# A recurrence and a mixture of experts on one core: the downs six units behind the ups, a rebuilt head, and five downs as three rounded passes

## What is computed

```python
xw = einsum('ntd,dh->nth', x, Wx) + b                 # 32 rows, 32 steps, 128 features
h_t = tanh(xw_t + h_(t-1) @ Wh)                       # a scan over the 32 steps
xf = h.reshape(-1, 128)                               # 1024 tokens
xn = xf * rsqrt(mean(xf * xf) + EPS) * norm_scale
vals, idx = top_k(xn @ wg + bg, 4)                    # 16 experts, 4 per token
gate = one_hot(idx) weighted by softmax(vals)
u = einsum('th,ehd->etd', xn, w1) + b1                # per expert: the up product
a, b = minimum(u[..., ::2], 7), clip(u[..., 1::2], -7, 7)
s = a * sigmoid(1.702 * a) * (b + 1)
y = einsum('eti,eih->eth', s, w2) + b2                # per expert: the down product
out = x + h + sum over e of gate[t, e] * y[e, t]
```

## Time and profile before

| | us |
|---|---|
| median of three runs | 108.16 |
| profiled execution | 107.47 |
| its span, first to last instruction | 105.7 |
| TensorE busy | 98.3 (93%) |
| VectorE, ScalarE, GpSimd busy | 67.2, 61.7, 64.7 |
| TensorE's share of the chain that ended last | 82% |

### The profile page before, as it was taken

One profiled execution on the slowest core, in us unless ns is written; L12 is line 12 of the kernel. 1 busy time (PEld: TensorE's weight loads), 2 busy tenths in 40 slices (PEclk: granted clock), 3 DMA queues, 4 the chain that ended last, 5 costly groups with the idle time before them and its releaser, 6 DMA issues.

```text
span 105.7 us, 1704 instructions
## 1 busy us (share of the span) xinstructions
PE 98.3 (93%) x549; PEld 83.6 (79%) x549; DVE 67.2 (64%) x179; ACT 61.7 (58%) x143; POOL 64.7 (61%) x77
## 2 busy tenths in 40 slices
PE   7778899989999999999999979999999999999980
PEld 2557789978999999999999958888777777777660
DVE  0302357976827996589787997668566556666740
ACT  3354836999755586667736646666555666655400
POOL 6004447997890995639963799689544566544400
PEclk9999999999999999999999999999999999999999
DMA  2999920007930000895048911995100000000003
GB/s 66 224 378 338 374 92 0 0 9 254 398 147 3 0 6 6 212 372 212 5 141 228 366 67 20 274 364 207 34 6 0 3 0 0 0 0 0 0 0 99
DMA packets 5000, 12.97 MB, mean 123 GB/s; under 512 B 752, under 2 KB 1792, under 8 KB 4992
## 3 DMA queue, kind: packets, MB, share of 16 engines
q1 hardware_dynamic: 4672, 12.69, 35.5%
q10 hardware_dynamic: 320, 0.18, 0.6%
HBM read 12.28 MB, written 0.59 MB: 122 GB/s over the span
## 4 chain that ended last, share of the span: by engine, by line
PE 82%; ACT 7%; DMA 2%; DVE 2%; POOL 2%; issue 2%; POOLq 0%; DVEq 0%; ACTq 0%
PE psA L806 20%; PE psB L806 19%; PE psY L836 12%; PE psR L836 7%; PE psR L753 5%; PE psY L753 3%; PE psM L836 3%; PE psR L848 2%; DMA wx_x_sb<-in_wx_x 2%; PE psR L745 2%; PE psM L760 2%; ACT small_h L450 2%; ACT psA L494 2%; PE psM L767 1%; ACT psA L503 1%
## 5 line engine op out<-in xcount | busy, mean ns | idle before, releaser
L414 POOL TENSOR_TENSOR actg<-act,gate_cols 128x512 f32<-128x512 f32 x31 | 39.4, 1281 | 12.5 <-DVE act L713 10.7
L696 DVE TENSOR_SCALAR lin<-psB,one_b1b 128x256 f32<-128x256 f32 (+1 forms) x48 | 26.0, 568 | 18.8 <-PE psB L806 18.8
L494 ACT ACTIVATE psA<-psA,lim_b1a 128x256 f32<-128x256 f32 (+1 forms) x48 | 23.8, 513 | 23.2 <-PE psA L806 23.1
L713 DVE SCALAR_TENSOR_TENSOR act<-lin,psA 128x512 f32<-128x512 f32 x32 | 22.0, 686 | 1.8 <-ACT psA L503 0.6
L503 ACT ACTIVATE psA<-psA,limit_col 128x512 f32<-128x512 f32 x32 | 21.1, 659 | 0.8
L806 PE MATMUL psA<-xn_hi,w_hi 128*128 128x256 f32 (+1 forms) x48 | 18.9, 394 | 0.2
L836 PE MATMUL psY<-actg,w_sb 128*128 128x256 f32 x64 | 17.2, 391 | 0.8 <-POOL actg L414 0.8
L806 PE MATMUL psB<-xn_hi,w_hi 128*128 128x256 f32 (+1 forms) x48 | 16.0, 333 | 0.0
L806 PE MATMUL psB<-xn_lo,w_hi 128*128 128x256 f32 (+1 forms) x48 | 15.6, 324 | 0.0
L806 PE MATMUL psB<-xn_hi,w_lo 128*128 128x256 f32 (+1 forms) x48 | 15.5, 323 | 0.0
L806 PE MATMUL psA<-xn_hi,w_lo 128*128 128x256 f32 (+1 forms) x48 | 15.5, 323 | 0.0
(11 more groups left out here) (87 smaller groups left out, 133.7 us busy)
## 6 DMA issues: line engine op xcount, KB each, us to landing
gate_cols<-gate_rows SPq DMA_DIRECT2D x16, 512.0 KB, 5.7
w_sb<-in_w SPq DMA_DIRECT2D x4, 512.0 KB, 7.3
w_sb<-in_w SPq DMA_DIRECT2D x4, 256.0 KB, 8.3
wx_x_sb<-in_wx_x SPq DMA_DIRECT2D x1, 320.0 KB, 5.9
wx_x_sb<-in_wx_x SPq DMA_DIRECT2D x2, 128.0 KB, 2.7
out<-yT SPq DMA_DIRECT2D x2, 128.0 KB, 4.3
out<-yT SPq DMA_DIRECT2D x1, 192.0 KB, 1.9
small_h<-in_small ACTq DMA_DIRECT2D x1, 105.0 KB, 2.8
```

Of the source, the lines that this page charges most:

```text
L414: nc.gpsimd.tensor_tensor(by_pair(actg[:, u % SUM_DEPTH, w]), by_pair(act[:, u % ACT_DEPTH, w]), gate_block(u, w), ALU.mult).then_inc(actg ...
L494: last = nc.scalar.activation(psA[u % 2][:, o], psA[u % 2][:, o], ACT.Relu, scale=-1.0, bias=lim_b1a[:, e0 + k:e0 + k + 1])
L696: last = nc.vector.tensor_scalar(lin[:, v % 2, o], psB[v % 2][:, o], one_b1b[:, e0 + k:e0 + k + 1], LIMIT + 1.0, ALU.add, ALU.min)
L713: nc.vector.scalar_tensor_tensor(act[:, v % ACT_DEPTH, 0:w], lin[:, v % 2, 0:w], 1.0 - LIMIT, psA[v % 2][:, 0:w], ALU.max, ALU.mult).then_ ...
```

## The change

`LAG` goes from 4 to 6, `POOL_LAG` from 2 to 3, and the buffers of `act` and `actg` from 6 and 5 to 8 and 6. With this, `add_h` of chunk 0 and the first down of chunk 1 move from slot 12 to slot 14, and the tail has six downs. The tail's two rounds are 256 and 256 columns where they were 384 and 128.

In the head, tile 1's x·Wx goes to `psX`, as do its sums of squares, with semaphores of their own. The products of tiles 1 to 6 are issued in the head (in steps' shadows or around the sums); only tile 7 comes later, in slot 10, where tiles 5 to 7 came together in slot 6. ScalarE rounds all of w1 before unit 0. In the first six slots the gate transposes and ScalarE's gate copies stand earlier in their slots. `gates_scale` is two scalar multiplications in place of one tensor product.

In units 17, 19, 21, 23 and 25 the down is three passes of fp32r operands. ScalarE rounds `actg` to `act_hi` at the head of slot u + 5 and GpSimd forms `act_lo` in the same slot, one before the down. The w2 parts of these five experts are made in slots 7 and 10 (ScalarE) and 8 and 11 (GpSimd).

```diff
-    LAG = 4
-    POOL_LAG = 2
-    ACT_DEPTH, SUM_DEPTH = 6, 5
+    LAG = 6
+    POOL_LAG = 3
+    ACT_DEPTH, SUM_DEPTH = 8, 6
...
-    W1_AHEAD, W1_SHARED = 5, 3
-    XW_AT = [0, 0, 1, 1, 2, 1, 2, 3]
-    XW_LATE = 5
+    W1_SHARED = 3
+    XW_AT = [0, 3, 0, 1, 2, 1, 2, 3]
+    XW_LATE = 7
...
+    SPLIT = list(range(UNIT0[NC - 1] + 1, NU - LAG, 2))
+    W2_HIGH, W2_LOW = [7, 10], [8, 11]
+    W2_PARTS = [0, 3, len(SPLIT)]
...
         def y_end(k):
-            o = [slice(0, 3 * P), slice(3 * P, W)][k]
+            o = [slice(0, PW), slice(PW, W)][k]
...
             def power_rstd(g):
-                pool.wait_ge(m_read, psM_turn(("stats", g)))
+                if g == 1:
+                    pool.wait_ge(mean_ready, 1)
+                else:
+                    pool.wait_ge(m_read, psM_turn(("stats", g)))
...
+            def act_low(u):
+                i = SPLIT.index(u)
+                pool.wait_ge(act_hi_ready, i + 1)
+                if i >= 2:
+                    pool.wait_ge(y_mm, SPLIT[i - 2] + 1)
+                nc.gpsimd.tensor_tensor(act_lo[:, i % 2, :], actg[:, u % SUM_DEPTH, :], act_hi[:, i % 2, :].bitcast(F32),
+                                        ALU.subtract).then_inc(act_lo_ready, 1)
+            def w2_low(i):
...
+                if v >= POOL_LAG:
+                    gate_product(v - POOL_LAG)
+                if v - LAG + 1 in SPLIT:
+                    act_low(v - LAG + 1)
+                for i in at(W2_LOW, v):
+                    w2_low(i)
                 for q in at(RSTD, v):
                     power_expo(q)
                     place_expo(q)
-                if v >= POOL_LAG:
-                    gate_product(v - POOL_LAG)
...
+            def act_high(u):
+                i = SPLIT.index(u)
+                acte.wait_ge(actg_done, u + 1)
+                if i >= 2:
+                    acte.wait_ge(y_mm, SPLIT[i - 2] + 1)
+                nc.scalar.activation(act_hi[:, i % 2, :], actg[:, u % SUM_DEPTH, :], ACT.Copy).then_inc(act_hi_ready, 1)
...
-            for k in range(HEAD - W1_AT - 2, 2 * W1_AHEAD):
+            for k in range(HEAD - W1_AT - 2, 2 * NP):
                 w1_high(k)
             for u in range(NU):
+                if u - LAG + 1 in SPLIT:
+                    act_high(u - LAG + 1)
...
+                if u < LAG:
+                    for q in at(GATES_T, u):
+                        copy_gates(q)
                 acte.wait_ge(relu_done, u + 1)
...
-                if u + W1_AHEAD < NP:
-                    w1_high(2 * (u + W1_AHEAD))
-                    w1_high(2 * (u + W1_AHEAD) + 1)
+                for i in at(W2_HIGH, u):
+                    w2_high(i)
...
             def sums(g):
                 pe.wait_ge(sq_ready, g + 1)
-                turn(("stats", g))
+                if g != 1:
+                    turn(("stats", g))
+                bank = psX if g == 1 else psM
...
+                if u in SPLIT:
+                    i = SPLIT.index(u)
+                    pe.wait_ge(w2_lo_ready, (i >= W2_PARTS[1]) + 1)
+                    passes = ((w2_hi, act_hi), (w2_lo, act_hi), (w2_hi, act_lo))
+                    for m, (w, x_part) in enumerate(passes):
+                        if m == 2:
+                            pe.wait_ge(act_lo_ready, i + 1)
+                        else:
+                            pe.wait_ge(act_hi_ready, i + 1)
+                        for o, y in y_parts(c):
+                            last = nc.tensor.matmul(y, w[:, i, :], x_part[:, i % 2, o], start=False, stop=False)
+                    last.then_inc(y_mm, 1)
+                    return
...
             for t in range(HEAD):
                 step(t)
-                if t == 3:
-                    x_wx(1, 1)
+                if t in (1, 2):
+                    x_wx(t, 1)
+                elif t == TL:
+                    x_wx(3, 1)
                 elif t == TL + 1:
                     pe.wait_ge(consts_ready, 1)
                     sums(0).then_inc(m_mm, 1)
                 elif t == TL + 2:
-                    pe.wait_ge(wg_ready, 1)
-                    raw_logits(range(0, 1), psB[0])
+                    x_wx(4, 1, start=False)
                 elif t == HEAD - 1:
                     lay_rstd(0)
-                    x_wx(2, 1)
-            sums(1).then_inc(m_mm, 1)
-            raw_logits(range(1, 2), psB[0]).then_inc(raw_mm, 1)
-            pe.wait_ge(step_done, HEAD)
-            x_wx(3, 1)
+            x_wx(5, 1, start=False)
+            sums(1).then_inc(sum1_mm, 1)
+            pe.wait_ge(wg_ready, 1)
+            raw_logits(range(0, 2), psB[0]).then_inc(raw_mm, 1)
             lay_rstd(1)
-            x_wx(4, 1, start=False)
+            x_wx(6, 1, start=False)
```

More of the change, by code:

```diff
@@ L140, in adaln_rnn_moe_kernel @@
         actg = sb("actg", [P, SUM_DEPTH, W])
+        act_hi = sb("act_hi", [P, 2, W], F32R)
+        act_lo = sb("act_lo", [P, 2, W], F32R)
+        w2_hi = sb("w2_hi", [P, len(SPLIT), H], F32R)
+        w2_lo = sb("w2_lo", [P, len(SPLIT), H], F32R)
         yT = sb("yT", [P, NT * P])
@@ L278, in xw_cols @@
             k = XW_AT[j]
-            return (psY if j in (0, 2) else psR)[:, k * P:(k + n) * P]
+            return (psX if j == 1 else psY if j in (0, 3, 4) else psR)[:, k * P:(k + n) * P]
         def step_psum(t):
@@ L289, in psM_turn @@
         def psM_turn(what):
-            order = [(k, g) for g in range(last_group(0) + 1) for k in ("stats", "rstd")]
+            order = [("stats", 0), ("rstd", 0), ("rstd", 1)]
             later = []
@@ L469, in copy_gates, with w2_high @@
                 nc.scalar.activation(gS[:, qc], psX[0:GR, 0:PW], ACT.Copy).then_inc(gS_high, 1)
+            def act_high(u):
[4 more added lines that the diff above has]
+                nc.scalar.activation(act_hi[:, i % 2, :], actg[:, u % SUM_DEPTH, :], ACT.Copy).then_inc(act_hi_ready, 1)
+            def w2_high(i):
+                to, es = w2_split(i)
+                for g in range(NG):
+                    acte.wait_ge(w2_loaded[g], 16)
+                nc.scalar.activation(w2_hi[:, to, :], w2_sb[:, es, :], ACT.Copy).then_inc(w2_hi_ready, 1)
             acte.wait_ge(small_loaded, 16)
@@ L506, in _ @@
                     tanh(t)
[L507 to L508 removed]
+                if u >= LAG:
+                    for q in at(GATES_T, u):
+                        copy_gates(q)
                 for q in at(STATS, u + 1):
                     square(pair_group(q))
[L511 to L513 removed]
+                for i in at(W2_HIGH, u):
+                    w2_high(i)
             acte.wait_ge(yT_ready, NC + 1)
[L515 removed]
+            store(acte, slice((NT - 2) * P, NT * P), slice(P // 2, P))
         @block.vector
@@ L530, in stats @@
                 n = len(ts)
-                dve.wait_ge(m_mm, psM_turn(("stats", g)))
-                mean = nc.vector.tensor_scalar(meansq[:, ts.start:ts.stop], psM[:, 0:n], 1.0 / H, EPS, ALU.mult,
-                                               ALU.add)
+                if g == 1:
+                    dve.wait_ge(sum1_mm, 1)
+                else:
+                    dve.wait_ge(m_mm, psM_turn(("stats", g)))
+                mean = nc.vector.tensor_scalar(meansq[:, ts.start:ts.stop], (psX if g == 1 else psM)[:, 0:n], 1.0 / H, EPS,
+                                               ALU.mult, ALU.add)
                 if g < CHUNKS[0]:
-                    mean.then_inc(m_read, 1)
+                    mean.then_inc(mean_ready if g else m_read, 1)
                 else:
@@ L618, in gates_scale @@
                 settled()
[L619 to L624, removed]
+                for j in pair_tiles(q):
+                    last = nc.vector.tensor_scalar(
+                        gates_w[:, j, :].rearrange("p (a b e) -> p a b e", a=3, b=2)[:, :, 0, :],
+                        gate_sum[:, j, :].rearrange("p (a e) -> p a e", a=1).to_broadcast([P, 3, E]),
+                        inv[:, j:j + 1], None, ALU.mult)
+                last.then_inc(scale_done, 1)
             def gates_low(q):
@@ L751, in step @@
                 if t == TL * XW_LATE:
-                    x_wx(XW_LATE, NT - XW_LATE)
+                    x_wx(XW_LATE, NT - XW_LATE, start=False)
                 nc.tensor.matmul(step_psum(t), wh_sb, hT[:, t * N:(t + 1) * N], start=False, stop=True,
@@ L757, in sums @@
                 pe.wait_ge(sq_ready, g + 1)
-                turn(("stats", g))
+                if g != 1:
+                    turn(("stats", g))
+                bank = psX if g == 1 else psM
                 for k, j in enumerate(group_tiles(g)):
-                    last = nc.tensor.matmul(psM[:, k:k + 1], sq[:, j * P:(j + 1) * P], ones[:, :], start=True, stop=True)
+                    last = nc.tensor.matmul(bank[:, k:k + 1], sq[:, j * P:(j + 1) * P], ones[:, :], start=True, stop=True)
                 return last
@@ L886, in _ @@
                         step(t)
+                    for q in at(GATES_T, v):
+                        transpose_gates(q)
```

(3 more changed lines are left out.)

16 lines of the change are left out of this document (15 added, 1 removed).

## The result

The changed kernel takes 112.73 us (median of four, 112.11 to 116.32) against 108.35 in the same session: ratio 1.039 (1.030 to 1.047). The ratios leave out executions, like that of 116.32, in which the chip was in a second, slower state. Run again later it took 112.13, ratio 1.041 (1.038 to 1.044). The forecast was 107.1 with a range from 106.0 to 108.3: a gain was expected, and the kernel lost. The profiled execution took 112.11 us, span 110.3.

What follows compares the result with a forecast made beforehand. TensorE, busy 14.80 of 14.80 us from 28.20 to 43.00, was taken as the bound there. Terms -1.1 + 0.21 - 0.15 + 0.43 - 0.8 + 0.35 = -1.06 gave 107.1 us from the median 108.16, range 106.0 to 108.3.

Steps and rivals of the forecast that it cites:

- the one on up(8): Slots 6 and 7: with two downs fewer ahead, up(8) comes at 35.7, a gain of 1.1, despite a new wait on act(6).
- the boundary: Start of chunk 1, slot 14: TensorE waits 1.29 us for add_h before down(8); net +0.43 at up(16), bounds -0.13 and +0.6.
- add_h late: Slot 14: add_h, behind VectorE's routing of the last pair, releases TensorE at about 59.73, while TensorE wants the down at 58.44.
- Rival 2: Up to up(8): the routing chain sets the pace and hides the early gain, 1.1 shrinks to 0.3: 107.9, no change; chance 0.21.
- Head: Before up(0): tile 1's sum of squares no longer waits for its bank, so up(0) starts about 0.35 earlier, at 14.76.
- w1's roundings ahead: Slots 0 to 4: roundings leave the recurrence; up(4) at 24.75 against 25.66, gain 0.9, of which 0.75 remains at up(5).
- The split: Last chunk: five fp32 downs become six rounded 256-column passes, 0.71 for 0.87; 0.16 saved each, 0.8 in all, bounds 0.5 and 0.9.
- rival 3: Last chunk: GpSimd becomes the bound because act_lo takes longer than twice the 256-column row; 109.9 at 2.3 us; chance 0.07.
- The tail: After unit 30's up: down 0.2 late behind the last act_lo, last addition about +0.13; sum +0.35.
- I let the rise come 0.35 earlier with up(0): Head: TensorE's clock rise moves 0.35 earlier with up(0); if not, half the 0.35 stays lost and the sum is 107.3.

Runs made afterwards that it cites:

- the shorter pause: Changed kernel with add_h earlier and GpSimd waiting for the scaled gates only behind xn_lo, ahead of the gate products: 106.65 us, ratio 0.984 to the kernel before.
- GpSimd waiting: Changed kernel, two scaling operations kept, with GpSimd waiting behind its product of the exponentials until that pair's gates are scaled: 106.93 us, ratio 0.984 to the kernel before.
- the last experiment: Changed kernel with old GpSimd order, one scaling operation and earlier add_h, but ScalarE's last six w1 roundings back between tanhs of slots 0 to 2: 107.51 us, ratio 0.992.
- the best version: Changed kernel with GpSimd's order of before, one tensor_tensor for the scaling, and add_h ahead of its slot's routing: 106.32 us, ratio 0.982 to the kernel before.

## Why the prediction was wrong

The step that failed is the one on up(8): "act(6) ends some 0.2 after TensorE is ready (bounds 0 and 0.7)". It took VectorE's list as it was before, in which the scaling of the gates takes 0.42, into a program in which GpSimd does something else at that moment. The two edits behind it had no term in the sum: the scaling's second operation, and GpSimd's gate product ahead of the exponentials. TensorE waited there for the gates, 1.68 us, and act(6), queued behind the scaling, ended only at 38.75. The same cause struck at two more places: slot 11 (1.14 of wait), and the boundary, where "add_h late" was priced but not the gates of the last pair behind it (0.66, and 0.26 on act at up(16)).

Slot 0 has a scaling of 1.49 too, and up(4) came at 25.88 (forecast 24.75), but most of that is the clock. In the kernel with the shorter pause (scaling 0.41) the last long pass also starts 4.62 behind up(0), and there up(4) is 10.82 behind up(0), here 10.99: the scaling cost 0.2. Against that same profile, whose clock rose as late, the changed kernel loses 2.0 from up(4) to up(8), 1.5 to up(12), 1.8 to up(16) (0.4 of it by the late addition), and nothing behind that.

Rival 2 named the place: the routing chain did set up(8), and the gain of 1.1 was gone. But it had no cause for a longer chain, and its price of 107.9 was far too low.

The four combinations show that the loss is these two edits together: two operations in the new order 112.13, two in the old order 109.09, one in the new order 108.75, one in the old order 106.97. From the last, the second operation alone costs 2.1, the order alone 1.8, both 5.2. (The 108.75 is from the earlier session; by ratio the four are 1.041, 1.012, 1.002, 0.993, so the order alone costs 0.9%, at the edge of the noise.) The profiles say the same without chip and clock: from up(4) to up(16) TensorE takes 35.84 with neither edit, 1.57 more with the second operation, 1.31 more with the order, 4.52 more with both. Together they cost more than their sum, since two operations in the new order wait for two gate products.

Why an operation on VectorE ends with one on GpSimd, the runs show only from outside. The scaling does so beside GpSimd's subtractions of 256 columns and products of 512, and not when GpSimd stands still. Other operations between SBUF tiles show it too: the two `logits` at 45.89 in the changed kernel take 0.75 beside a gate product (0.37 elsewhere), xn_hi at 61.73 takes 0.45 (0.29). Reductions, the reciprocal and operations that read PSUM (lin, act) keep their time. So does `hot`, with both inputs in SBUF, beside GpSimd's exponential of six columns: 0.29 in every profile.

```profile
33.18 1.32 POOL L398 TENSOR_TENSOR expo<-euler,diff 128x6 f32<-128x6 f32 x1 [0.87 <-DVE diff L653]
```

```profile
33.64 0.29 DVE L666 TENSOR_TENSOR hot<-iota_e,top_f 128x128 f32<-128x128 f32 x1
```

The Trainium skill, SBUF — State Buffer, section "Who interferes with whom", gives a reason: the two engines share one pair of SBUF ports, held for a whole instruction, and a tensor_scalar that uses both ports, or a VectorE operation with two SBUF inputs beside a GpSimd one that reads SBUF, blocks if it issues second. The traces agree in both forms: 2.22 us for two of the first, 1.07 for one of the second, beside gate products of 1.25. By that rule the forecast should have walked through every VectorE operation with SBUF inputs that the new GpSimd order moves.

In slot 0 GpSimd is the one that waits: the single operation starts 0.02 ahead of a w_lo and takes 0.26, and that w_lo takes 0.83, its neighbours 0.73. Two rows do not fit, and there the measurement decides: `hot` beside the exponential, and the first tensor_scalar of slot 0, which starts 0.02 ahead of a w_lo in the changed kernel and still takes 0.80.

The other steps, measured where nothing holds the scaling up (GpSimd waiting; its profile has a span of 104.8 and a time of 106.6, against the 106.4 that the forecast gives for the profiled execution; its last long pass starts 2.92 behind up(0), as in the profile before):

- Head: up(0) at 14.62 to 15.27 in the twelve profiles with the new head (forecast 14.76, before 15.11), the squares' sum without a wait. Right in kind, but the executions differ by more than the 0.35 of the gain.
- w1's roundings ahead: up(4) at 24.78 (24.75), up(5) at 27.53 (27.6, which is 29.47 before, less 1.12 for the first down with its correction product and less the 0.75). Right at these places. By the last experiment the roundings are worth 0.5 to 0.7 at up(5), but only 0.35 at up(4), where 0.9 was forecast.
- up(8): 36.05 (35.7). Right in kind, 0.35 too early: by the starts, slot 7 loses 0.28 ahead of the transposes and 0.28 ahead of up(8), where the forecast had 0.2 for both.
- The boundary: a wait of 1.29 on yT (1.29), and from up(14) to up(16) 6.48 against 5.85 before, so +0.63 (63.41 less 62.78, also 0.63). Right. The addition placed earlier gives 0.44 of it back.
- The split: 0.16 a unit (0.16), 0.68 in all (0.8). Right. GpSimd's act_lo takes 1.28 (1.47 forecast): rival 3 was far off.
- The tail: right within 0.05. From the first round to the end it takes 8.61 in the changed kernel, 6.59 before; less two more downs of 0.86 that is +0.3 (+0.35). In the changed kernel the two rounds of six half downs start 2.66 apart (101.71, 104.37), against six times 0.43, 2.58: 0.1 of wait, not 0.2. The last addition takes 0.42 (0.41), and what follows it 0.1 more than before.

So the forecast of 107.1, 0.990 of the median before, is the time of the change without its two unpriced edits (106.97, ratio 0.993). Its sum holds there within its bounds, and its list of edits was not complete: the rivals asked which engine becomes full or which chain sets the pace, none what an engine off the path does to its neighbour's durations.

## What to carry to other kernels

A duration read from a trace holds for what ran beside it there. When an edit reorders GpSimd, lay its new rows against VectorE's. For each elementwise VectorE operation between SBUF tiles that falls beside a GpSimd product or subtraction of 128 columns or more, count the rest of the GpSimd operation, once per instruction; reductions and operations that read PSUM were not held up here. A small operation that ends within 0.15 us behind an operation on the other engine, and is several times longer than where that engine stands still, is a wait booked as work. Here a semaphore wait on the engine with time to spare removed it.

## What the runs showed of the hardware

The moment at which TensorE's clock rises differs between executions, by some 0.6 us between two of the changed kernel; in the twelve profiles with the new head the last long pass starts 2.5 to 4.6 behind up(0). I read the upper level, 2.4 GHz, from passes of 0.28 and the lower, 1.2 GHz, from passes of 0.41; the clock column of the changed kernel shows 1.00 over both. In the best version they change before up(1); with the shorter pause in the middle of it. TensorE's rows there:

```profile
17.58 0.41 PE L873 MATMUL psB<-xn_lo,w_hi 128*128 128x256 f32 x1
...
18.18 0.28 PE L873 MATMUL psA<-xn_hi,w_lo 128*128 128x256 f32 x1
```

```profile
19.89 0.41 PE L876 MATMUL psA<-xn_lo,w_hi 128*128 128x256 f32 x1
...
20.99 0.28 PE L876 MATMUL psB<-xn_hi,w_lo 128*128 128x256 f32 x1
```

up(2) follows at 20.32 and 21.73, up(8) at 36.09 and 37.12; the profiled times are 106.06 and 107.09. Of this 1.0, 0.6 is there at up(0) already: in the head the steps at 4.86 and 5.65 take 0.41 in the first profile, those at 4.85 and 5.87 take 0.64 in the second. The later rise itself is worth 0.8 at up(2) and 0.4 at up(8). Over 0 to 15 us the clock column shows 0.76 in the first and 1.00 in the second. It reads 0.75 or 0.76 in four of the twelve profiles with the new head, and in these the last long pass starts earliest, at 17.3 to 17.6. So a lower mean there goes with an earlier rise and with short steps in the head; why is open. The executions of the kernel with w1 between the tanhs fall into two groups of times, 106.70 to 106.97 and 107.49 to 107.79; the mean granted clock is 0.951 or 1.000 in the four of the first group and 0.995 to 0.999 in the eight of the second. So the groups go with the clock; which stretch makes the difference is not shown. The Trainium skill, TensorE: Matmul & The Clock Gate, section "What's actually happening", says that the gate's window runs free of the kernel's start; the last long passes start between 17.3 and 19.9 with up(0) at 14.62 to 15.27, which agrees with it; and the forecast's step "I let the rise come 0.35 earlier with up(0)" has no ground.

The scaling itself, with GpSimd still, takes 0.41 as two operations; as one, where it started just ahead of a GpSimd operation, 0.26. Of GpSimd's operations the exponential of six columns holds nothing up. What else does not stays open: one that only writes SBUF was not tried.
